# High and low parts of the attention values in one matmul of 130 columns

## The chip, the cores and the metric

The kernel runs on one core of a Trainium2 chip. The metric is the device time in microseconds (us) of one execution, given as the median of several runs. Four engines compute: TensorE (PE in the profile, its weight loads PEld), VectorE (DVE), ScalarE (ACT) and GpSimd (POOL). SyncE (SP) only issues DMAs.

## What is computed

Eight graphs of 2048 nodes, one layer of graph attention with 8 heads of 64 outputs, a residual and a layer norm:

```python
h = einsum('bnf,hfo->bhno', x, W)            # x: 8 x 2048 x 512, W: 8 x 512 x 64
s1 = einsum('bhno,ho->bhn', h, a1)
s2 = einsum('bhno,ho->bhn', h, a2)
e = leaky_relu(s1[..., :, None] + s2[..., None, :], negative_slope=0.2)
attn = softmax(where(adj > 0, e, -9e15), axis=-1)
out = layernorm(x + concat_heads(einsum('bhnm,bhmo->bhno', attn, h)))
```

Since exp(leaky_relu(s1+s2)) is a product of a factor of the row and a factor of the column on either side of s1+s2 = 0, the kernel needs no exponential per edge. It needs two masks per head, the edges with s1+s2 > 0 ("pos") and the other edges ("neg"), and multiplies each by a table with 65 columns per head: 64 scaled values and the denominator.

## The kernel before, in words

A **unit** is one head of one block of 512 rows. A batch has 4 blocks (k) of 8 heads (h), so 32 units, and there are 8 batches, 256 units in all. A unit has IT = 4 row tiles of 128 and JC = 16 column chunks of 128.

The tables exist as a high and a low f16 part, to keep precision: `b_hi`, `b_lo` for pos and `d_hi`, `d_lo` for neg.

What each engine does for a unit:

- **ScalarE** (L505 to L520, `compare`): copies the row scores to a PSUM bank (L510), then 13 comparisons of 128x512 (L519) into the two `step` tiles, 6 for the first half of the columns and 7 for the second. There is one pair of `step` tiles, so the comparisons of unit u+1 into a half begin when VectorE has used that half for unit u. In between it cuts adjacency pieces (L487, 8 per block: all in h = 0 of block 0, else two in h = 0 and one in h = 1 to 6) and copies transposed x tiles (L493, 16 per batch).
- **VectorE** (loop at L797 to L828): in iteration u it makes 3 comparisons (L707) and both masks of unit u+1: `make_pos` twice (L722, AND of half a mask), `make_neg` twice (L731, XOR of half a mask); then in some units a maximum (L567) or other small work; then `take_unit(u)` (L571 to L581): scale the neg sums out of PSUM (L576), add the pos sums (L579), invert the denominators (L581); then in h = 1 to 3 parts of the layer norm. Everything stands in this order in one queue. In unit 0 of a batch no masks are made (those of unit 1 were made in the batch's start).
- **TensorE** (L430 to L477): waits for the pos masks, and per row tile multiplies one tiny term (L448, 65 columns) and for each of 16 mask tiles the high part (L454) and the low part (L455), each a weight load of the mask tile and a matmul of 65 columns, all summed in the same 65 columns of a PSUM bank. Then in some units x transposes or score products (L368, L378, L386, L393, L399), then it waits for the neg masks and does the same without the tiny term (L475, L476). There are two sets of banks, by the parity of h, so pos of unit u+1 needs unit u-1 to have been read (`unit_read`).
- **GpSimd** divides the result of the unit by its denominator (L871, L876), adds x by DMA and does small parts of the norm.

A batch starts with 16 chunks of x times W (L429, f32), which VectorE scales and splits (L693 to L698) and GpSimd completes (L915, L917).

## Time and profile before

| | us |
|---|---|
| median of 3 runs | 3147.84 |
| lowest, highest | 3135.4, 3163.03 |
| the profiled execution's own time | 3138.42 |
| its span | 3136.7 |
| TensorE busy | 2744.1 |
| VectorE busy | 2522.8 |
| ScalarE busy | 2419.3 |
| GpSimd busy | 827.5 |

The span is counted from the first to the last instruction, the own time is that of the same execution as the runs measure it. "Busy" of TensorE is the union of matmuls that overlap one another, so a matmul's mean duration (195 ns) is far more than the distance between two of them. "issue" in a wait is time in which an engine waited for no semaphore that the profile shows. The mean granted clock of TensorE is 0.967 of full speed.

### The profile page before, as it was taken

To read this page: it belongs to the slowest core of one execution; us is meant where nothing else is said; L and a number is where in the kernel's file an instruction comes from. 1 tells how busy PE (TensorE), PEld (TensorE's weight loads), DVE (VectorE), ACT (ScalarE), POOL (GpSimd) and SP (SyncE) were. 2 spreads that over 40 slices of the span, in tenths; PEclk is the share of its full clock that TensorE was granted. 3 is DMA by queue.
4 is the path that set the end of the run, shared out by engine and by line. 5 is a ranking of instruction groups with operands and counts; after the bars stand their busy time and mean duration, and the time that the engine had idled before them with its cause. 6 is when DMAs were issued, how large, how long until landed. Compare 5 with 4: busy or idle time off the path is not lost.

```text
span 3136.7 us, 158793 instructions
## 1 busy us (share of the span) xinstructions
PE 2744.1 (87%) x68636; PEld 2398.0 (76%) x68636; DVE 2522.8 (80%) x3954; ACT 2419.3 (77%) x4029; POOL 827.5 (26%) x1011
## 2 busy tenths in 40 slices
PE   4898889998898898988989889998898888988886
PEld 2498876988678885888858888498884888758886
DVE  4888878887887878888788787888877877788876
ACT  2499973999658996599856998479973989739994
POOL 2522115111341113312142111521215111161211
PEclk9999999999999999999999999999999999999998
DMA  5357643576526655277442765437644556345753
GB/s 162 93 116 161 141 100 100 123 164 131 130 71 136 150 130 136 63 157 157 111 118 70 159 155 122 98 88 165 150 108 115 112 143 156 90 112 115 165 135 94
DMA packets 281338, 392.28 MB, mean 125 GB/s; under 512 B 161856, under 2 KB 161856, under 8 KB 280672
## 3 DMA queue, kind: packets, MB, share of 16 engines
q1 hardware_dynamic: 253536, 315.24, 39.9%
q0 software_dynamic: 27136, 67.12, 12.7%
q8 instruction: 545, 8.93, 1.2%
q14 instruction: 121, 0.99, 0.2%
HBM read 313.52 MB, written 34.14 MB: 111 GB/s over the span
## 4 chain that ended last, share of the span: by engine, by line
PE 67%; issue 13%; DVE 10%; ACT 7%; DMA 1%; SPq 1%; POOL 0%; DVEq 0%; ACTq 0%; POOLq 0%
PE ps L475 14%; PE ps L476 14%; PE ps L455 13%; PE ps L454 13%; PE ps L429 8%; ACT step L519 7%; PE ps L368 2%; DVE m_neg L731 1%; DVE y L603 1%; PE ps L386 1%; PE ps L399 1%; DVE prod L695 1%; PE ps L448 1%; DVE prod_d L698 1%; DVE m_pos L722 1%
## 5 line engine op out<-in xcount | busy, mean ns | idle before, releaser
L519 ACT ACTIVATE step<-ps,s_steep 128x512 fp8e4<-128x512 f32 x3328 | 1954.1, 726 | 289.7 <-DVE m_pos L722 246.9
L455 PE MATMUL ps<-b_lo,m_pos 128*128 128x65 f16 x16384 | 1094.3, 195 | 96.4 <-issue 95.4
L454 PE MATMUL ps<-b_hi,m_pos 128*128 128x65 f16 x16384 | 1093.7, 195 | 54.4 <-issue 36.5
L475 PE MATMUL ps<-d_hi,m_neg 128*128 128x65 f16 x16384 | 1071.9, 195 | 67.0 <-issue 61.2
L455 PEld LDWEIGHTS ps<-b_lo,m_pos 128*128 128x128 fp8e5 x16384 | 1052.3, 98 | 101.3 <-issue 101.0
L475 PEld LDWEIGHTS ps<-d_hi,m_neg 128*128 128x128 fp8e5 x16384 | 1043.6, 99 | 98.5 <-issue 97.9
L476 PE MATMUL ps<-d_lo,m_neg 128*128 128x65 f16 x16384 | 1072.7, 195 | 42.3 <-issue 42.1
L454 PEld LDWEIGHTS ps<-b_hi,m_pos 128*128 128x128 fp8e5 x16384 | 1052.5, 98 | 66.3 <-issue 66.1
L476 PEld LDWEIGHTS ps<-d_lo,m_neg 128*128 128x128 fp8e5 x16384 | 1039.1, 99 | 34.9 <-issue 33.3
L722 DVE TENSOR_TENSOR m_pos<-step,maskT 128x1024 uint32<-128x1024 uint32 x512 | 623.8, 1242 | 163.4 <-ACT step L519 130.6
L731 DVE TENSOR_TENSOR m_neg<-m_pos,maskT 128x1024 uint32<-128x1024 uint32 x512 | 602.8, 1217 | 0.0
L429 PE MATMUL ps<-W_sb,xT 128*128 128x512 f32 x1024 | 464.1, 615 | 61.5 <-DVE prod_d L698 54.7
L871 POOL TENSOR_TENSOR den_scaled<-den_inv,bound 128x4 f32<-128x4 f32 x256 | 74.9, 292 | 1592.0 <-DVE den_inv L581 1533.9
L429 PEld LDWEIGHTS ps<-W_sb,xT 128*128 128x128 f32 x1024 | 200.8, 198 | 319.3 <-issue 240.6
L707 DVE TENSOR_SCALAR step<-s_bc,s_neg 128x512 fp8e5<-128x512 f32 x768 | 391.1, 565 | 12.4 <-DVE s_neg L666 3.6
L487 ACT ACTIVATE adj_cut<-adj_in 128x1024 fp8e4<-128x1024 int32 x264 | 291.1, 1132 | 120.0 <-DMA adj_in<-in_adj 120.0
L576 DVE TENSOR_TENSOR neg_part<-ps,r_row 128x260 f32<-128x260 f32 x256 | 108.8, 425 | 316.3 <-PE ps L476 315.8
L493 ACT ACTIVATE xT<-ps 128x512 f32<-128x512 f32 x144 | 96.9, 673 | 175.8 <-PE ps L368 175.8
L510 ACT ACTIVATE ps<-s_bc 128x512 f32<-128x512 f32 x256 | 174.6, 682 | 71.9 <-DVE s_neg L666 71.4
L876 POOL TENSOR_TENSOR y<-total,den_scaled 128x256 f32<-128x256 f32 x256 | 206.2, 805 | 22.7 <-POOL den_scaled L871 2.3
L448 PE MATMUL ps<-tiny,ones_bf 128*128 128x65 bf16 x1024 | 199.0, 194 | 11.2 <-issue 6.3
L917 POOL TENSOR_TENSOR d_lo<-prod_d,d_hi 128x512 f16<-128x512 f32 x128 | 176.2, 1376 | 9.0
(81 smaller groups left out, 1703.4 us busy)
## 6 DMA issues: line engine op xcount, KB each, us to landing
adj_in<-in_adj SPq DMA_DIRECT2D x266, 512.0 KB, 4.8
s_bc<-s_rows SPq DMA_DIRECT2D x258, 256.0 KB, 3.8
x_in<-in_x SPq DMA_DIRECT2D x144, 256.0 KB, 4.7
x_sum<-in_x POOLq DMA_DIRECT2D x128, 256.0 KB, 4.6
y<-in_x POOLq DMA_DIRECT2D x32, 1024.0 KB, 10.4
out<-y SPq DMA_DIRECT2D x32, 1024.0 KB, 7.4
maskT<-adj_cut SPq DMA_TRANSPOSE x264, 4.3
W_sb<-in_L_gnn_W SPq DMA_DIRECT2D x4, 256.0 KB, 6.8
```

Source lines behind the costliest of these rows:

```text
L429: mm = pe.matmul(ps[:, H_BANKS[jc % 3], :], xT[:, fc, jc * P:(jc + 1) * P], W_sb[:, fc, :], start=(fc == 0), stop=(fc == FC - 1))
L448: pe.matmul(acc, ones_bf[:], tiny[:, h, :], start=True, stop=False)
L454: pe.matmul(acc, mask, b_hi[:, j, h, :], start=False, stop=False)
L455: mm = pe.matmul(acc, mask, b_lo[:, j, h, :], start=False, stop=(j == JC - 1))
L475: pe.matmul(acc, mask, d_hi[:, j, h, :], start=(j == 0), stop=False)
L476: mm = pe.matmul(acc, mask, d_lo[:, j, h, :], start=False, stop=(j == JC - 1))
L487: nc.scalar.activation(adj_cut8[slot][:], adj_in[slot][:], ACT.Relu, scale=STEEP, saturate=False).then_inc(adj_cut, 1)
L519: ins = nc.scalar.activation(chunk(step[qd], c, 0, BLK), ps[:, BANK_S1, :], ACT.Relu, bias=s2_steep[:, j, h:h + 1], scale=STEEP, saturate= ...
L707: ins = V.tensor_scalar(chunk(step[qd], c, 0, BLK).bitcast(FP8_WIDE), s1_bc[hp][:], s2_neg[:, j, h:h + 1], STEP_UP, ALU.is_gt, ALU.mult, s ...
L722: V.tensor_tensor(words(m_pos[hp][:, js, :]), words(step[qd][:]), words(mask[:, js, :]), ALU.bitwise_and).then_inc(pos_made, 1)
L731: V.tensor_tensor(words(m_neg[hp][:, js, :]), words(m_pos[hp][:, js, :]), words(mask[:, js, :]), ALU.bitwise_xor).then_inc(neg_made, 1)
L876: G.tensor_tensor(y[par][:, :, h * O:(h + 1) * O], total[hp][:, :, 0:O], den_scaled[hp][:].unsqueeze(2).to_broadcast([P, IT, O]), ALU.mult ...
```

## The change

High and low part of a table lie next to each other in one tile (`b_both`, `d_both`: 2 x 65 columns per head). One matmul of 130 columns per mask tile takes the place of two of 65, and leaves the high and the low sum in neighbouring slots of a PSUM bank. VectorE adds the two sums with a reduction over a pair whose members lie 65 elements apart: pos by `take_pos`, between the pos and the neg mask of the next unit, neg at the head of `take_neg`. Scaling and adding then run from SBUF. A bank holds two slots of 130 columns, so pos takes banks 0 and 1 and neg banks 2 and 3, one set for all units: pos of unit u+1 needs pos of unit u read (`pos_read`), likewise neg (`neg_read`). The neg mask is one XOR of 2048 words instead of two of 1024, at both places where it is made.

```diff
--- before
+++ after
@@ -110,10 +110,11 @@
         BANK_X = 6
-        b_hi = sb("b_hi", [P, JC, H, O1], F16)
-        b_lo = sb("b_lo", [P, JC, H, O1], F16)
-        d_hi = sb("d_hi", [P, JC, H, O1], F16)
-        d_lo = sb("d_lo", [P, JC, H, O1], F16)
+        b_both = sb("b_both", [P, JC, H, 2, O1], F16)
+        d_both = sb("d_both", [P, JC, H, 2, O1], F16)
+        b_hi, b_lo = b_both[:, :, :, 0, :], b_both[:, :, :, 1, :]
+        d_hi, d_lo = d_both[:, :, :, 0, :], d_both[:, :, :, 1, :]
         maskT = [sb(f"maskT{i}", [P, JC // 2, 2 * BLK], FP8) for i in range(2)]
         m_pos = [sb(f"m_pos{i}", [P, JC // 2, 2 * BLK], FP8) for i in range(2)]
...
@@ -222,10 +223,12 @@
         step_dve = sem("step_dve", free=1)
         pos_made = sem("pos_made", free=QUADS)
         neg_made = sem("neg_made", free=0)
+        pos_read = sem("pos_read", free=0)
+        neg_read = sem("neg_read", free=0)
         unit_done = sem("unit_done", free=1)
         pos_summed = sem("pos_summed", free=1)
         neg_scaled = sem("neg_scaled")
-        unit_read = sem("unit_read", free=1)
+        total_made = sem("total_made")
         den_inverted = sem("den_inverted")
         den_made = sem("den_made")
         att_made = sem("att_made", free=1)
...
@@ -244,6 +247,16 @@
         def pairs(ap):
             return ap.bitcast(BF16)
+        S = 2 * O1
+        def slot(bank, it):
+            return ps[:, bank + it // 2, it % 2 * S:(it % 2 + 1) * S]
+        def slots(bank):
+            return ps[:, bank:bank + 2, 0:2 * S].rearrange("p k (t l c) -> p k t c l", t=2, l=2)
         def chunk(tile, j, i0, n):
...
@@ -442,17 +455,19 @@
                             pe.wait_ge(lo_made, at(lo_made, 2 * JC * (b + 1) - 2))
                         pe.wait_ge(pos_made, at(pos_made, QUADS * (u + 1)))
-                        pe.wait_ge(unit_read, at(unit_read, u - 1))
+                        pe.sem_inc(waited[pe.engine], 1)
+                        pe.wait_ge(pos_read, at(pos_read, u))
+                        pe.sem_inc(waited[pe.engine], 1)
                         for it in range(IT):
-                            acc = ps[:, 2 * hp, it * O1:(it + 1) * O1]
-                            pe.matmul(acc, ones_bf[:], tiny[:, h, :], start=True, stop=False)
+                            acc = slot(0, it)
                             for j in range(JC):
                                 if unit == 0 and it == 0 and j == JC - 1:
                                     pe.wait_ge(lo_made, at(lo_made, 2 * JC * (b + 1) - 1))
                                     pe.sem_inc(waited[pe.engine], 1)
                                 mask = chunk(m_pos[hp], j, it * P, P).bitcast(FP8_WIDE)
-                                pe.matmul(acc, mask, b_hi[:, j, h, :], start=False, stop=False)
-                                mm = pe.matmul(acc, mask, b_lo[:, j, h, :], start=False, stop=(j == JC - 1))
+                                mm = pe.matmul(acc, mask, b_both[:, j, h, :, :], start=(j == 0), stop=(j == JC - 1))
+                                if j == 0:
+                                    pe.matmul(acc[:, 0:O1], ones_bf[:], tiny[:, h, :], start=False, stop=False)
                         mm.then_inc(pos_summed, 1)
                         if unit == 0:
                             pe.wait_ge(lo_made, at(lo_made, 2 * JC * (b + 1)))
...
@@ -466,14 +481,15 @@
                         if unit == STURN_UNIT:
                             turn_scores(b + 1)
                             mean_h(b + 1)
-                        pe.wait_ge(neg_made, at(neg_made, QUADS * (u + 1)))
+                        pe.wait_ge(neg_made, at(neg_made, u + 1))
+                        pe.sem_inc(waited[pe.engine], 1)
+                        pe.wait_ge(neg_read, at(neg_read, u))
                         pe.sem_inc(waited[pe.engine], 1)
                         for it in range(IT):
-                            acc = ps[:, 2 * hp + 1, it * O1:(it + 1) * O1]
+                            acc = slot(2, it)
                             for j in range(JC):
                                 mask = chunk(m_neg[hp], j, it * P, P).bitcast(FP8_WIDE)
-                                pe.matmul(acc, mask, d_hi[:, j, h, :], start=(j == 0), stop=False)
-                                mm = pe.matmul(acc, mask, d_lo[:, j, h, :], start=False, stop=(j == JC - 1))
+                                mm = pe.matmul(acc, mask, d_both[:, j, h, :, :], start=(j == 0), stop=(j == JC - 1))
                         mm.then_inc(unit_done, 1)
...
@@ -567,17 +583,23 @@
                 V.tensor_reduce(xmax[:, col:col + 1], x_in[slot][:], AX.X, ALU.max,
                                 apply_absolute_value=True).then_inc(x_maxed, 1)
-            def take_unit(u, h, it0):
+            def take_pos(u, h):
                 hp = h % 2
-                pos = ps[:, 2 * hp, 0:IT * O1].rearrange("p (t c) -> p t c", t=IT)
-                neg = ps[:, 2 * hp + 1, 0:IT * O1].rearrange("p (t c) -> p t c", t=IT)
+                dve.wait_ge(pos_summed, at(pos_summed, u + 1))
+                dve.wait_ge(att_made, at(att_made, u - 1))
+                dve.sem_inc(waited[dve.engine], 1)
+                V.tensor_reduce(total[hp][:], slots(0), AX.X, ALU.add).then_inc(pos_read, 1)
+            def take_neg(u, h, it0):
+                hp = h % 2
                 r = r_row[:, it0:it0 + IT, h:h + 1].to_broadcast([P, IT, O1])
                 dve.wait_ge(unit_done, at(unit_done, u + 1))
-                V.tensor_tensor(neg_part[:], neg, r, ALU.mult).then_inc(neg_scaled, 1)
+                V.tensor_reduce(neg_part[:], slots(2), AX.X, ALU.add).then_inc(neg_read, 1)
+                dve.wait_ge(neg_read, at(neg_read, u + 1))
+                V.tensor_tensor(neg_part[:], neg_part[:], r, ALU.mult).then_inc(neg_scaled, 1)
                 dve.wait_ge(neg_scaled, u + 1)
-                dve.wait_ge(att_made, at(att_made, u - 1))
-                V.tensor_tensor(total[hp][:], pos, neg_part[:], ALU.add).then_inc(unit_read, 1)
-                dve.wait_ge(unit_read, at(unit_read, u + 1))
+                V.tensor_tensor(total[hp][:], total[hp][:], neg_part[:], ALU.add).then_inc(total_made, 1)
+                dve.wait_ge(total_made, u + 1)
                 V.reciprocal(den_inv[hp][:], total[hp][:, :, O]).then_inc(den_inverted, 1)
             def ln_first_half(g, par):
...
@@ -722,27 +744,28 @@
                 V.tensor_tensor(words(m_pos[hp][:, js, :]), words(step[qd][:]),
                                 words(mask[:, js, :]), ALU.bitwise_and).then_inc(pos_made, 1)
-            def make_neg(u, h, mask, qd):
+            def make_neg(u, h, mask):
                 hp = h % 2
-                if qd == 0:
-                    dve.wait_ge(unit_done, at(unit_done, u - 1))
-                js = slice(qd * JQ // 2, (qd + 1) * JQ // 2)
-                dve.wait_ge(pos_made, at(pos_made, QUADS * u + qd + 1))
-                V.tensor_tensor(words(m_neg[hp][:, js, :]), words(m_pos[hp][:, js, :]),
-                                words(mask[:, js, :]), ALU.bitwise_xor).then_inc(neg_made, 1)
-            def make_masks(u, h, mask, nth, first_of_block=None):
+                dve.wait_ge(unit_done, at(unit_done, u - 1))
+                dve.wait_ge(pos_made, at(pos_made, QUADS * (u + 1)))
+                V.tensor_tensor(words(m_neg[hp][:]), words(m_pos[hp][:]), words(mask[:]), ALU.bitwise_xor
+                                ).then_inc(neg_made, 1)
+            def make_masks(u, h, mask, nth, first_of_block=None, before=None):
                 compare(h, nth)
                 for qd in range(QUADS):
                     make_pos(u, h, mask, qd, first_of_block)
-                for qd in range(QUADS):
-                    make_neg(u, h, mask, qd)
+                if before is not None:
+                    take_pos(u - 1, before)
+                make_neg(u, h, mask)
             V.nop().then_inc(x_maxed, start[x_maxed])
             V.nop().then_inc(step_dve, start[step_dve])
             V.nop().then_inc(pos_made, start[pos_made])
             V.nop().then_inc(neg_made, start[neg_made])
-            V.nop().then_inc(unit_read, start[unit_read])
+            V.nop().then_inc(pos_read, start[pos_read])
+            V.nop().then_inc(neg_read, start[neg_read])
             V.memset(ones_bf[:], 1.0).then_inc(ones_bf_made, 1)
             V.memset(wa[:], 0.0)
             V.memset(tiny_f[:], TINY * SPLIT_TOP).then_inc(setup_step, 1)
...
@@ -804,10 +827,13 @@
                             dve.sem_inc(waited[dve.engine], 1)
                             with dve.If(b < B - 1):
                                 make_masks(u + 1, 0, maskT[0], (g + 1) * (H // 2), g + 1)
+                            take_pos(u, h)
                         elif h == H - 1:
-                            make_masks(u + 1, 0, maskT[(k + 1) % 2], (g + 1) * (H // 2), g + 1)
+                            make_masks(u + 1, 0, maskT[(k + 1) % 2], (g + 1) * (H // 2), g + 1, before=h)
                         elif unit > 0:
-                            make_masks(u + 1, h + 1, maskT[k % 2], g * (H // 2) + (h + 1) // 2)
+                            make_masks(u + 1, h + 1, maskT[k % 2], g * (H // 2) + (h + 1) // 2, before=h)
+                        else:
+                            take_pos(u, h)
                         if unit in TILE_UNIT:
                             t = TILE_UNIT.index(unit)
                             max_x(JC * (b + 1) + t, t % 2, (b + 1) * (JC // 2) + t // 2, t)
...
@@ -823,7 +849,7 @@
                             no_edge_part(b + 1, 0)
                             no_edge_part(b + 1, 1)
                             no_edge_part(b + 1, 2)
-                        take_unit(u, h, k * IT)
+                        take_neg(u, h, k * IT)
                         for when, work in ((1, ln_first_half), (2, ln_statistics), (3, ln_apply)):
                             if h == when and k:
                                 work(g - 1, (k - 1) % 2)
```

VectorE, an iteration of the block loop that has a maximum in it, before (rows as the program lists them; ISA and REGISTER_ALU are waits and register steps of the queue):

```order
L722 TENSOR_TENSOR m_pos<-step,maskT 128x1024
L720 REGISTER_ALU
L722 TENSOR_TENSOR m_pos<-step,maskT 128x1024
L731 TENSOR_TENSOR m_neg<-m_pos,maskT 128x1024 x2
L566 ISA
L567 TENSOR_REDUCE xmax<-x_in 128x1
L576 TENSOR_TENSOR neg_part<-ps,r_row 128x260
L579 TENSOR_TENSOR total<-ps,neg_part 128x260
L581 RECIPROCAL den_inv<-total 128x4
```

The same place in the changed kernel:

```order
L744 TENSOR_TENSOR m_pos<-step,maskT 128x1024
L742 REGISTER_ALU
L744 TENSOR_TENSOR m_pos<-step,maskT 128x1024
L591 TENSOR_REDUCE total<-ps 128x260
L750 ISA
L751 TENSOR_TENSOR m_neg<-m_pos,maskT 128x2048
L582 ISA
L583 TENSOR_REDUCE xmax<-x_in 128x1
L597 TENSOR_REDUCE neg_part<-ps 128x260
L599 TENSOR_TENSOR neg_part<-neg_part,r_row 128x260
L601 TENSOR_TENSOR total<-total,neg_part 128x260
L603 RECIPROCAL den_inv<-total 128x4
```

Two reductions are new in the queue, one of them ahead of the XOR, and the two XORs are one.

TensorE, from the last pos matmuls of a unit with an x transpose to its first neg matmuls, before:

```order
L454 MATMUL ps<-b_hi,m_pos 128x65
L455 MATMUL ps<-b_lo,m_pos 128x65
L365 REGISTER_ALU
L368 MATMUL ps<-ident,x_in 128x128 x4
L469 REGISTER_ALU
L475 MATMUL ps<-d_hi,m_neg 128x65
L476 MATMUL ps<-d_lo,m_neg 128x65
```

The same place in the changed kernel, on to the next unit's pos:

```order
L470 MATMUL ps<-tiny,ones_bf 128x65
L468 MATMUL ps<-b_both,m_pos 128x130 x15
L378 REGISTER_ALU
L381 MATMUL ps<-ident,x_in 128x128 x4
L484 REGISTER_ALU
L492 MATMUL ps<-d_both,m_neg 128x130 x64
L457 ISA
L468 MATMUL ps<-b_both,m_pos 128x130
```

The pairs of 65 columns are single matmuls of 130, 64 for each mask of a unit; the tiny term now comes second in its row tile.

## Rows read from the trace of the kernel before

**Rows 1.** The page: span; busy us, share and instructions of each engine.

```profile
span 3136.7 us, 158793 instructions
PE 2744.1 (87%) x68636; PEld 2398.0 (76%) x68636; DVE 2522.8 (80%) x3954; ACT 2419.3 (77%) x4029; POOL 827.5 (26%) x1011
```

**Rows 2.** The page: shares of the chain of waits, by engine.

```profile
PE 67%; issue 13%; DVE 10%; ACT 7%; DMA 1%; SPq 1%; POOL 0%; DVEq 0%; ACTq 0%; POOLq 0%
```

**Rows 3.** Waits of the whole run: who for whom, us, times, longest.

```profile
DVE neg_part L576 <- PE ps L476: 315.8, 154, 8.2
...
ACT step L519 <- DVE m_pos L722: 246.9, 101, 15.8
...
DVE m_pos L722 <- ACT step L519: 130.6, 103, 2.9
...
PE ps L455 <- issue: 95.4, 75, 3.4
```

**Rows 4.** Windows of one batch: start, units 1-7 of block 0, blocks 1, 2, 3.

```profile
core 0: us, PE busy (x) PEld busy (x) DVE busy (x) ACT busy (x) POOL busy (x), PEclk, DMA share, GB/s
1208.97:1275.05 66.08, 58.28 (x132) 25.62 (x133) 56.52 (x96) 32.22 (x50) 41.22 (x35) 0.95 0.45 112
...
1287.16:1348.00 60.84, 59.62 (x1895) 59.20 (x1891) 55.19 (x79) 54.75 (x94) 10.33 (x18) 1.00 0.32 76
1348.00:1428.00 80.00, 67.71 (x2012) 66.31 (x2009) 63.68 (x95) 73.59 (x123) 15.57 (x23) 0.96 0.68 154
1428.00:1508.00 80.00, 69.98 (x2088) 68.51 (x2085) 65.17 (x99) 74.73 (x126) 15.66 (x23) 0.96 0.69 150
1508.00:1597.00 89.00, 81.49 (x2211) 72.98 (x2208) 68.04 (x118) 69.97 (x120) 14.36 (x20) 0.98 0.48 108
```

**Rows 5.** Timeline of VectorE, one unit of block 0: start us, us, instruction, idle before.

```profile
1295.67 0.43 DVE L576 TENSOR_TENSOR neg_part<-ps,r_row 128x260 f32<-128x260 f32 x1 [0.27 <-PE ps L476]
1296.13 0.43 DVE L579 TENSOR_TENSOR total<-ps,neg_part 128x260 f32<-128x260 f32 x1
1296.60 0.18 DVE L581 RECIPROCAL den_inv<-total 128x4 f32<-128x4 f32 x1
1296.73 1.64 DVE L707 TENSOR_SCALAR step<-s_bc,s_neg 128x512 fp8e5<-128x512 f32 x3
1298.51 2.36 DVE L722 TENSOR_TENSOR m_pos<-step,maskT 128x1024 uint32<-128x1024 uint32 x2
1300.79 2.35 DVE L731 TENSOR_TENSOR m_neg<-m_pos,maskT 128x1024 uint32<-128x1024 uint32 x2
1303.47 0.43 DVE L576 TENSOR_TENSOR neg_part<-ps,r_row 128x260 f32<-128x260 f32 x1 [0.33 <-PE ps L476]
```

**Rows 6.** Timeline of ScalarE in the same block.

```profile
1300.41 7.63 ACT L519 ACTIVATE step<-ps,s_steep 128x512 fp8e4<-128x512 f32 x13 [0.28 <-ACT ps L510]
1308.08 0.60 ACT L510 ACTIVATE ps<-s_bc 128x512 f32<-128x512 f32 x1
1308.96 7.63 ACT L519 ACTIVATE step<-ps,s_steep 128x512 fp8e4<-128x512 f32 x13 [0.28 <-ACT ps L510]
```

**Rows 7.** TensorE: two matmul groups of the page.

```profile
L454 PE MATMUL ps<-b_hi,m_pos 128*128 128x65 f16 x16384 | 1093.7, 195 | 54.4 <-issue 36.5
L448 PE MATMUL ps<-tiny,ones_bf 128*128 128x65 bf16 x1024 | 199.0, 194 | 11.2 <-issue 6.3
```

**Rows 8.** Windows of ten us in which TensorE stalled, recovered and ran full.

```profile
1130.00:1140.00 10.00, 6.54 (x183) 6.33 (x180) 5.81 (x6) 9.72 (x17) 2.19 (x3) 0.98 0.95 190
1140.00:1150.00 10.00, 9.89 (x192) 7.11 (x189) 8.16 (x14) 8.92 (x16) 0.81 (x2) 0.85 0.85 140
1150.00:1160.00 10.00, 10.00 (x333) 10.00 (x334) 5.73 (x11) 6.18 (x11) 0.82 (x2) 1.00 0.17 45
```

**Rows 9.** The page: the queue that brings instructions (packets, MB, share).

```profile
q8 instruction: 545, 8.93, 1.2%
```

**Rows 10.** Groups of VectorE reductions and f32 additions: busy us, mean ns.

```profile
L567 DVE TENSOR_REDUCE xmax<-x_in 128x1 f32<-128x512 f32 x144 | 97.6, 677 | 25.5 <-DMA x_in<-in_x 25.5
...
L657 DVE TENSOR_TENSOR tiny_f<-tiny_f,tiny_part 128x520 f32<-128x520 f32 x18 | 12.4, 692 | 0.0
...
L621 DVE TENSOR_REDUCE stat<-s_col 128x8 f32<-128x128 f32 x9 | 3.4, 373 | 1.1
...
L622 DVE TENSOR_REDUCE stat<-xmax 128x1 f32<-128x16 f32 x9 | 1.4, 158 | 0.0
...
L772 DVE TENSOR_REDUCE w_norm<-ps 128x1 f32<-128x512 f32 x1 | 0.7, 692 | 3.4 <-PE ps L412 3.4
```

**Rows 11.** Timeline of VectorE: masks over a batch's end, and its unit 0.

```profile
1212.51 1.22 DVE L722 TENSOR_TENSOR m_pos<-step,maskT 128x1024 uint32<-128x1024 uint32 x1 [2.94 <-ACT step L519]
1216.56 1.23 DVE L722 TENSOR_TENSOR m_pos<-step,maskT 128x1024 uint32<-128x1024 uint32 x1 [2.83 <-ACT step L519]
...
1287.20 0.43 DVE L576 TENSOR_TENSOR neg_part<-ps,r_row 128x260 f32<-128x260 f32 x1 [8.25 <-PE ps L476]
```

6 lines of the change are left out of this document (3 added, 3 removed).

## The prediction, made before the change was run

> **What bounds the kernel now.** I read the page first: TensorE is busy for 87% of the span, VectorE for 80%, ScalarE for 77% [rows 1], and the chain of waits runs through TensorE for 67% [rows 2]. So no engine has much room, and the question is which waits end last. The list of waits answers it: VectorE stands 315.8 us before `take_unit` for TensorE, and 130.6 us before the pos masks for ScalarE; ScalarE stands 246.9 us for VectorE's pos masks [rows 3]. The three form one loop. TensorE holds VectorE up in `take_unit`, and because that stands ahead of the next masks in VectorE's queue, ScalarE and then TensorE are held too.
>
> The windows show the loop by stage. In units 1 to 7 of a batch TensorE is busy for 59.62 of 60.84 us, VectorE for 55.19, ScalarE for 54.75. In blocks 1 to 3 TensorE does 67.71, 69.98 and 81.49 us in 80, 80 and 89, VectorE 63.68, 65.17 and 68.04 [rows 4]. TensorE's missing time there is stalls by "issue": 95.4 us before the low pos matmuls alone [rows 3], and they fall where DMAs are thick (183 matmuls in ten us at a DMA share of 0.95, against 333 at 0.17) [rows 8]. TensorE reads 8.93 MB of instructions through its own queue [rows 9], and I take late instructions for the cause.
>
> **What the change does to TensorE.** A full window holds 333 matmuls of 65 columns, 30.0 ns from one to the next [rows 8]; the mean of 195 ns in the groups is each one's way through the engine, several at once, and no cost [rows 7]. At 2.4 GHz (granted clock 1.00 in that row) 65 columns are 27.1 ns, so 2.9 ns is fixed. One matmul of 130 columns has as bounds 54.2 ns (no fixed part) and 60.0 (two of the old); I take 57.1. A unit of 260 x 30.0 = 7.8 us becomes 128 x 57.1 + 4 x 30.0 = 7.4 us: 0.4 us less. It has 132 weight loads and as many matmuls where there were 260 of each, so the stalls should about halve.
>
> On fetching, the Trainium skill (Runtime: NRT & Kernel Launch, Instruction fetch mechanics) says that instructions come in blocks of 16 KiB and that the cost is mostly hidden. The size agrees (8.93 MB in 545 packets), "hidden" does not agree with the 95.4 us in one line. By that rule the change would be worth 0.4 us a unit on TensorE at most.
>
> **What it does to VectorE.** Step by step for one unit:
>
> - *Two reductions added.* Each reads 520 f32 from PSUM and writes 260. A reduction of 512 costs 0.692 us from PSUM and 0.677 from SBUF [rows 10]; with 8 more elements I take 0.70. The lower bound is 520 elements at 1.04 ns, 0.54 us, and a small overhead: 0.60. The upper bound comes from the one reduction with far strides: 128 elements, 16 x 4 bytes apart, cost 373 ns, while 16 next to each other cost 158 [rows 10]. With an overhead of 158 - 16 x 1.04 = 141 ns that is 1.81 ns an element, and 520 of them cost 1.08 us. Pos is followed by an instruction that waits for nothing and starts some 0.08 us before its end (as the second XOR does: two of 1.22 us in 2.35), so it takes 0.62. Neg is followed by its reader: 0.70 + 0.04 = 0.74.
> - *Scale and add from SBUF.* Now 0.43 us each from PSUM [rows 5]. The f32 addition of 520 from SBUF costs 0.692 [rows 10], so 260 cost 0.42. Nothing gained or lost.
> - *One XOR for two.* The pair takes 2.27 us to the next start; one of 2048 words should take 1.22 + 1024 x 1.04 ns = 2.28 less the overlap of 0.08. Gain 0.07.
>
> The sum is 0.62 + 0.74 - 0.07 = **1.29 us a unit, 330 us in 256 units**. The pos reduction of a batch's unit 0 lies within a wait of 8.25 us [rows 11], so 5 us of it are free: 325.
>
> A unit of block 0 is 7.80 us from one `take_unit` to the next with 0.33 us of waiting [rows 5], so 7.47 of work; it becomes 8.76. ScalarE's own round there is 8.56 us (1300.41 to 1308.96) [rows 6], TensorE's 7.4 to 7.8. **VectorE becomes the bound.**
>
> **What of it is absorbed.** VectorE waits 315.8 + 130.6 = 446.4 us for TensorE and ScalarE now [rows 3]. Not all of that is open to it. In each batch 8.25 us before unit 0 is TensorE's work after a serial start, and 2.94 + 2.83 us at the end is ScalarE, which cannot begin unit 0 of the next batch before VectorE has its scores [rows 11]: 14.0 x 8 = 112 us stay. The other 334 us are waits that VectorE reaches later by the added work. Of them I leave 30 us standing, where block 3 has score products of 512 columns on TensorE (81.49 us busy [rows 4]) and ScalarE cuts two pieces. So 304 go, 325 come: +21 us. TensorE's unit 0 is shorter by 0.4 x 8 = 3: **+18 us**.
>
> The windows give the same from another side. Units 1 to 7 have 55.19 + 7 x 1.29 = 64.2 us of VectorE work and some 2 us of gaps, 66 for 60.84: 5 us longer. Block 1 has 63.68 + 10.3 + 4 of gaps = 78, block 2 79.5, for 80: 2.5 shorter. Block 3, 68.04 + 10.3 + 4 + 5.8 = 88 for 89: 1 shorter. That is 1.5 us a batch, 12 in all.
>
> The single bank set costs nothing in this: pos of unit u+1 now waits for `take_pos(u)`, 0.62 us behind the pos masks that it waits for anyway, and TensorE has over 1 us in each unit to give. Neg of unit u+1 needs `take_neg(u)`'s first reduction, 2.9 us behind that, and pos takes 3.7. Behind the waiting `take_pos` in VectorE's queue stands the XOR, which TensorE needs only after those 3.7 us.
>
> The profiled execution took 3138.4 us, 1.7 more than its span; with +18 it is 3156. The median of the runs stands 9.4 above it, so I forecast **3166 us**.
>
> **Rivals.**
>
> 1. *Balanced, as above*: 3166, 50%. Its own range is 3120 to 3215 (reductions 0.62 to 0.74, 0 to 80 us of waits left).
> 2. *The pair is slow to read*, 33%. The two members lie 65 elements apart, so no two successive reads are neighbours. At 1.08 us a reduction costs 0.38 more, twice a unit, 195 us, and since VectorE is the bound all of it is paid: 3361. For it speaks the reduction of 373 ns [rows 10]. Against it: that one reads SBUF, and no row shows a strided read of PSUM. It decides from 0.73 us a reduction, where the rise of 18 passes 31 us, 1%. The Trainium skill (SBUF — State Buffer, the note on cachelines) says that a stride past a line of 16 bytes pays a penalty in SBUF, and that PSUM has lines of 8 bytes, two f32. By it the pair would pay at every element; the SBUF row agrees, no row shows PSUM.
> 3. *Faster*, 12%. The stalls of TensorE spread further than the waits I counted: the small gaps between VectorE's instructions, about 4 us in a block, are partly waits too short to be listed. If half of them (2 x 4 x 8 = 64 us) and the 30 I left went as well, the result is 3072; half of that effect, 3120.
> 4. *TensorE's clock falls*, 5%. It idles over 1 us in every unit now. The clock fell to 0.85 on average in the ten us after a stall [rows 8]. At 1.2 GHz for a third of each unit TensorE needs about 9 us, and the six units of a batch with other TensorE work then come last, 1.5 us each: +72, 3238.
>
> The range reaches from part of 3 to the whole of 2: 3110 to 3375. What a measurement here can tell from no change is about 1%, 31 us. Of case 1's 50%, 28 lie within that, 3 below and 19 above; of case 3's 12%, 9 are faster and 3 within; of case 2's 33%, 3 are so cheap that they stay within, 30 are slower, as are the 5 of case 4. So faster 12%, same 34%, slower 54%. The likeliest case itself is "no change".
>
> **What would show it.** Right: VectorE busy at about 2850 us; its wait for TensorE before the neg reduction down to little more than 66 us (unit 0); TensorE busy shares down and its chain share taken by VectorE; matmuls of 130 columns 57 ns apart; instruction traffic near 5 MB; the reductions at 0.70 us. Units 1 to 7 longer, the later blocks not. Wrong: reductions of 1 us or more (case 2); VectorE still waiting some 200 us for TensorE, with TensorE full at a low granted clock (case 4); or a wait of TensorE for `pos_read` in every unit while VectorE itself waits for ScalarE, which would mean that the single bank set has closed a loop that I called open.

## The result: no change that lasts, where 18 us more were forecast

The changed kernel takes 3128.9 us (median of 13 runs, 3126.1 to 3131.6), the kernel before beside it 3147.8 (13 runs, 3120.7 to 3163.4): ratio 0.9948, 95% interval 0.9925 to 0.9971. In a second comparison on another occasion the changed kernel takes 3128.0 (12 runs), the kernel before 3130.5 (17 runs): ratio 1.0015, 0.9989 to 1.0041. So where both ran side by side the change is worth between half a per cent and nothing, and not the 0.6% more that I forecast. The changed kernel hardly moves from run to run; the kernel before does. Ratios leave out the runs that lie more than 1.5% above the fastest of their kernel (six of the 17 in the second comparison), so they can differ a little from the quotient of the medians. On a third occasion, on another chip than that of the second comparison, the kernel before took 3097.8 us and the changed kernel was not run; if it is as steady there as the version of experiment 8 was (3087.4 us there, 3089.2 on the later occasion), it would be about 1% slower than the kernel before. That is an estimate from these numbers.

The page of the changed kernel: span, busy us of each engine, the instruction queue, the chain's shares.

```profile
span 3127.7 us, 94002 instructions
...
PE 2628.9 (84%) x35868; PEld 2276.5 (73%) x35868; DVE 2821.2 (90%) x4210; ACT 2419.8 (77%) x4029; POOL 822.5 (26%) x1011
...
q8 instruction: 296, 4.85, 0.7%
...
DVE 42%; ACT 18%; issue 18%; PE 18%; DMA 1%; DVEq 1%; POOL 1%; SPq 1%; ACTq 0%; POOLq 0%
```

Against [rows 1] VectorE is busy 298.4 us more and TensorE 115 us less. Against [rows 2] the chain has passed from TensorE (67%) to VectorE (42%). The instruction queue brings 4.85 MB where it was 8.93 [rows 9]. The list of waits (who for whom, us, times, longest):

```profile
PE ps L468 <- DVE total L591: 325.9, 210, 3.9
...
DVE m_pos L744 <- ACT step L535: 65.7, 63, 2.9
...
DVE total L591 <- PE ps L468: 36.9, 8, 5.1
...
DVE neg_part L597 <- PE ps L492: 20.1, 9, 2.8
...
PE ps L468 <- issue: 0.4, 1, 0.4
...
PE ps L492 <- issue: 0.2, 1, 0.2
```

VectorE's waits of 315.8 and 130.6 us [rows 3] are now 36.9 + 20.1 and 65.7. TensorE waits 325.9 us for the pos sum to be read, which is the slack that it now has. And the line that I had misjudged: TensorE's waits by "issue" inside its attention matmuls were 95.4 us on one line [rows 3] and 235.2 on all four. These are the other three in the kernel before:

```profile
PE ps L475 <- issue: 61.2, 43, 2.8
...
PE ps L476 <- issue: 42.1, 32, 3.2
...
PE ps L454 <- issue: 36.5, 41, 2.3
```

In the changed kernel they are 0.4 + 0.2 us. They do not hide in the wait for the pos sum either: in each of the 216 units in which the trace has TensorE idle until that sum is read, its pos matmuls start 0.15 us after the reduction's end.

The new operations, by group (busy us, mean ns, idle before):

```profile
L744 DVE TENSOR_TENSOR m_pos<-step,maskT 128x1024 uint32<-128x1024 uint32 x512 | 620.4, 1242 | 96.3 <-ACT step L535 65.7
L751 DVE TENSOR_TENSOR m_neg<-m_pos,maskT 128x2048 uint32<-128x2048 uint32 x256 | 584.1, 2281 | 0.4
...
L591 DVE TENSOR_REDUCE total<-ps 128x260 f32<-128x520 f32 x256 | 177.4, 693 | 47.0 <-PE ps L468 36.9 <-issue 9.4 <-DVE s_neg L688 0.7
L597 DVE TENSOR_REDUCE neg_part<-ps 128x260 f32<-128x520 f32 x256 | 176.9, 691 | 20.3 <-PE ps L492 20.1
L599 DVE TENSOR_TENSOR neg_part<-neg_part,r_row 128x260 f32<-128x260 f32 x256 | 109.8, 429 | 8.7
```

And one unit of block 0 on VectorE's timeline, the answer to [rows 5]:

```profile
1305.34 0.69 DVE L597 TENSOR_REDUCE neg_part<-ps 128x260 f32<-128x520 f32 x1
1306.07 0.43 DVE L599 TENSOR_TENSOR neg_part<-neg_part,r_row 128x260 f32<-128x260 f32 x1
1306.53 0.43 DVE L601 TENSOR_TENSOR total<-total,neg_part 128x260 f32<-128x260 f32 x1
1307.00 0.18 DVE L603 RECIPROCAL den_inv<-total 128x4 f32<-128x4 f32 x1
1307.22 1.67 DVE L729 TENSOR_SCALAR step<-s_bc,s_neg 128x512 fp8e5<-128x512 f32 x3
1309.01 2.36 DVE L744 TENSOR_TENSOR m_pos<-step,maskT 128x1024 uint32<-128x1024 uint32 x2
1311.29 0.69 DVE L591 TENSOR_REDUCE total<-ps 128x260 f32<-128x520 f32 x1
1311.89 2.28 DVE L751 TENSOR_TENSOR m_neg<-m_pos,maskT 128x2048 uint32<-128x2048 uint32 x1
```

Both reductions take 0.69 us. From start to start neg costs 0.73, pos 0.60 and the XOR 2.20. From the neg reduction at 1305.34 to the end of the XOR there is no wait left; the queue is full.

By stage, from the reading of the neg sums of unit 0 to that of units 7, 15, 23 and 31 of one batch. Before (stretch, its length, then busy us and instructions of PE, PEld, DVE, ACT, POOL; granted clock, DMA share, GB/s):

```profile
1287.20:1346.95 59.75, 58.53 (x1858) 58.11 (x1855) 54.21 (x75) 53.70 (x92) 10.33 (x18) 1.00 0.31 74
1346.95:1429.46 82.51, 70.22 (x2094) 68.82 (x2091) 65.68 (x99) 76.10 (x128) 15.57 (x23) 0.96 0.68 154
1429.46:1510.05 80.59, 70.58 (x2106) 69.10 (x2103) 65.74 (x99) 75.05 (x126) 15.66 (x23) 0.96 0.69 149
1510.05:1602.02 91.97, 84.24 (x2155) 72.75 (x2151) 69.87 (x120) 72.93 (x124) 14.36 (x20) 0.98 0.47 106
```

After:

```profile
1287.32:1351.22 63.90, 57.17 (x991) 56.24 (x988) 62.08 (x82) 55.72 (x96) 10.86 (x19) 1.00 0.33 78
1351.22:1429.33 78.11, 64.13 (x1080) 62.90 (x1078) 74.93 (x108) 74.74 (x126) 15.56 (x23) 0.98 0.65 157
1429.33:1507.58 78.25, 64.80 (x1070) 63.58 (x1068) 75.17 (x108) 74.87 (x126) 15.64 (x23) 0.96 0.62 153
1507.58:1599.22 91.64, 78.76 (x1098) 67.62 (x1095) 79.24 (x128) 73.10 (x124) 13.61 (x20) 0.96 0.41 104
```

Block 0 (first rows) is 4.2 us longer: there nobody had time to give, and VectorE's 62.08 of 63.90 us is the bound. In this batch blocks 1 and 2 are 4.4 and 2.3 us shorter although VectorE does 9.3 and 9.4 us more in them, and block 3 is 0.3 shorter with 9.4 more. Over all eight batches the means are 3.5 longer, then 3.4, 0.9 and 1.4 shorter. The lengths of the first three stages vary in the kernel before (block 1 from 77.7 to 84.8 us) and are the same to 0.02 us in every batch of the changed kernel. In blocks 1 and 2 ScalarE is as busy as VectorE (74.74 and 74.93 of 78.11 us), so there the two are the bound together.

### The profile page after: what moved, and what is told of

It reads as the page before. It is cut to its first block, busy times and chain, and to the rows that moved or that the text cites. A ratio compares the mean times of both kernels' runs of the same rounds, so it can differ in the third digit from the quotient of the medians.

```text
span 3127.7 us, 94002 instructions
## 1 busy us (share of the span) xinstructions
PE 2628.9 (84%) x35868; PEld 2276.5 (73%) x35868; DVE 2821.2 (90%) x4210; ACT 2419.8 (77%) x4029; POOL 822.5 (26%) x1011
## 3 DMA queue, kind: packets, MB, share of 16 engines
q8 instruction: 296, 4.85, 0.7%
## 4 chain that ended last, share of the span: by engine, by line
DVE 42%; ACT 18%; issue 18%; PE 18%; DMA 1%; DVEq 1%; POOL 1%; SPq 1%; ACTq 0%; POOLq 0%
ACT step L535 16%; DVE m_neg L751 10%; PE ps L442 7%; DVE m_pos L744 6%; PE ps L468 5%; DVE step L729 5%; PE ps L492 4%; DVE neg_part L597 3%; DVE total L591 2%; DVE neg_part L599 2%; DVE total L601 2%; DVE y L625 2%; DVE xmax L583 1%; ACT ps L526 1%; DVE ln_stats L612 1%
## 5 line engine op out<-in xcount | busy, mean ns | idle before, releaser
L468 PE MATMUL ps<-b_both,m_pos 128*128 128x130 f16 x16384 | 1075.3, 228 | 348.2 <-DVE total L591 325.9
L468 PEld LDWEIGHTS ps<-b_both,m_pos 128*128 128x128 fp8e5 x16384 | 1020.9, 102 | 382.7 <-issue 382.7
L492 PE MATMUL ps<-d_both,m_neg 128*128 128x130 f16 x16384 | 978.4, 221 | 26.2 <-DVE neg_part L597 25.9
L492 PEld LDWEIGHTS ps<-d_both,m_neg 128*128 128x128 fp8e5 x16384 | 952.0, 98 | 41.4 <-issue 40.0
L744 DVE TENSOR_TENSOR m_pos<-step,maskT 128x1024 uint32<-128x1024 uint32 x512 | 620.4, 1242 | 96.3 <-ACT step L535 65.7
L751 DVE TENSOR_TENSOR m_neg<-m_pos,maskT 128x2048 uint32<-128x2048 uint32 x256 | 584.1, 2281 | 0.4
L591 DVE TENSOR_REDUCE total<-ps 128x260 f32<-128x520 f32 x256 | 177.4, 693 | 47.0 <-PE ps L468 36.9
L597 DVE TENSOR_REDUCE neg_part<-ps 128x260 f32<-128x520 f32 x256 | 176.9, 691 | 20.3 <-PE ps L492 20.1
L943 POOL TENSOR_TENSOR d_both<-prod_d,d_both 128x512 f16<-128x512 f32 x128 | 177.4, 1386 | 9.0
L941 POOL TENSOR_TENSOR b_both<-prod,b_both 128x512 f16<-128x512 f32 x128 | 144.0, 1125 | 108.5 <-DVE prod L717 106.3
L875 POOL DMA_DIRECT2D x_sum<-in_x x128 | 118.5, 926 | 107.6 <-DMA x_sum<-in_x 99.0
```

The source lines that it names most:

```text
L468: mm = pe.matmul(acc, mask, b_both[:, j, h, :, :], start=(j == 0), stop=(j == JC - 1))
L492: mm = pe.matmul(acc, mask, d_both[:, j, h, :, :], start=(j == 0), stop=(j == JC - 1))
L591: V.tensor_reduce(total[hp][:], slots(0), AX.X, ALU.add).then_inc(pos_read, 1)
L597: V.tensor_reduce(neg_part[:], slots(2), AX.X, ALU.add).then_inc(neg_read, 1)
L744: V.tensor_tensor(words(m_pos[hp][:, js, :]), words(step[qd][:]), words(mask[:, js, :]), ALU.bitwise_and).then_inc(pos_made, 1)
L751: V.tensor_tensor(words(m_neg[hp][:]), words(m_pos[hp][:]), words(mask[:]), ALU.bitwise_xor).then_inc(neg_made, 1)
```

## Experiments

Times are medians. The kernel before is given beside each group, because it is what varies: 3097.8 us (17 runs) beside the first group (the 65-column matmuls, the high sums alone, the late pos sum, GpSimd), 3135.3 (23 runs) beside the second (the second reduction, the two XORs, and the two made from the kernel before), 3130.5 (17 runs) beside the third. The changed kernel was 3128.9 and 3128.0 on its two occasions; differences from it are taken from 3128.5. The changed kernel did not run beside the first group. There the kernel before was 1% faster than elsewhere, so a version of the first group whose time moves as that of the kernel before does (experiment 1) may cost more elsewhere than its difference says.

**1. TensorE's relief taken back.**

```diff
-                                mm = pe.matmul(acc, mask, b_both[:, j, h, :, :], start=(j == 0), stop=(j == JC - 1))
+                            for l in range(2): for j in range(JC):    # neg likewise
+                                mm = pe.matmul(acc[:, l * O1:(l + 1) * O1], mask, b_both[:, j, h, l, :], start=(j == 0), stop=(j == JC - 1))
```

> The changed kernel, but each row tile first multiplies its 16 mask tiles by the high parts and then by the low parts, 65 columns each, into the same two slots: TensorE has 260 matmuls a unit again, VectorE's work is the changed kernel's. Theory (VectorE sets the pace; TensorE now has about 1.2 us of slack a unit, into which its instruction stalls fall): TensorE needs 7.8 us a unit and stalls for some 240 us in all again, so part of the stalls no longer fits: 3140 to 3175 us, and the runs spread over more than 10 us as those of before do, not over 5. Rival (the gain comes from VectorE's new order alone, one read of PSUM earlier, and the wide matmul brings nothing): 3129 us, spread 5 us.

Measured 3237.9 us (3219.2 to 3246.6), 109 more than the changed kernel; ratio to before 1.0435 (1.038 to 1.049). VectorE's work is the same (2824.5 us busy, 2821.2 in the changed kernel). Its waits:

```profile
PE ps L469 <- issue: 167.2, 113, 4.0
...
DVE neg_part L601 <- PE ps L495: 125.9, 59, 5.6
...
PE ps L495 <- issue: 81.9, 64, 4.2
```

The stalls are back (249 us on the two lines) and VectorE waits 125.9 us for the neg sums instead of 20.1. The wide matmul is what makes the change bearable. My theory (3140 to 3175) gave it 12 to 47 us and is far too low; the rival (nothing) is wrong. The likely reason is that a slack of 1.2 us a unit does not take in stalls of up to 4 us, and that VectorE's full queue cannot make up what it lost; no run here separates that.

**2. VectorE's load alone, without the relief.**

```diff
                 dve.wait_ge(unit_done, at(unit_done, u + 1))   # take_unit of the kernel before
+                for i in range(2): V.tensor_reduce(spare[i][:], both, AX.X, ALU.add)
```

> The kernel before with two idle reductions of 520 PSUM elements into spare tiles at the head of VectorE's reading of a unit: VectorE's added work of the change, 1.3 us a unit, without any of TensorE's relief. Theory (the wide matmuls make room for it, because TensorE's 7.8 us and its stalls are shorter): slower than the changed kernel by more than 30 us, 3160 to 3260 us. Rival (VectorE's waits would have absorbed the reductions anyway): 3130 to 3150 us.

Measured 3250.1 us (3236.5 to 3261.6), ratio to before 1.0363 (1.0313 to 1.0413).

```profile
DVE spare L579 <- PE ps L477: 178.5, 58, 8.2
...
PE ps L456 <- issue: 109.8, 64, 4.2
...
PE ps L476 <- issue: 54.1, 47, 2.8
...
PE ps L455 <- issue: 36.4, 35, 2.8
...
DVE r_row L675 <- issue: 31.3, 7, 5.2
...
PE ps L477 <- issue: 24.3, 28, 2.5
```

This version is 115 us or 3.6% above the kernel before, for 295.4 us more busy time on VectorE (2818.2), with 224.6 us of stalls on the four lines of TensorE. Not all of the 115 us is the load's work in the loop. VectorE itself stands 31.3 us by "issue" before `r_row` in the starts of seven batches, where the kernel before has 4.3, and the way from the last reading of a batch to the first of the next is 71.8 us instead of 66.9, 34 us in seven starts. The cause of that is open. The loop pays the rest, about 80 us or 2.6%. The step from here to the changed kernel is -122 us, and -88 without the 34; experiment 1, whose starts are as short as the changed kernel's, gives 109 us for the relief. So the two halves of the change are each about 3% of the time and cancel. They are not independent: experiment 6 has TensorE's relief and little more work on VectorE (60.9 us), and is only 1.6% below the kernel before.

**3. The pos reduction twice.**

```diff
+                V.tensor_reduce(spare[:], slots(0), AX.X, ALU.add)
                 V.tensor_reduce(total[hp][:], slots(0), AX.X, ALU.add).then_inc(pos_read, 1)
```

> The changed kernel with the reduction of the pos sums done twice (once into a spare tile). Adds 0.61 us a unit on VectorE and nothing elsewhere. Theory (VectorE sets the pace, all of its work is paid): 255 x 0.61 = 156 less 5 for unit 0 of each batch: 3270 to 3285 us. Rival (VectorE's waits or another engine's loop pace it, so half or more is absorbed): under 3210 us.

Measured 3241.8 us (3240.6 to 3243.3), 113 more. The rival falls, and the theory's 3270 to 3285 is missed too: of the 151 us of work three quarters are paid, not all. The stages say where: block 0 becomes 4.2 us longer (63.90 to 68.14 us), which is all of 7 x 0.61; blocks 1 and 2 become 3.9 and 3.7 longer and block 3 2.4, each of 8 x 0.61 = 4.9 (means of eight batches).

**4. The XOR in halves again.**

```diff
-                V.tensor_tensor(words(m_neg[hp][:]), words(m_pos[hp][:]), words(mask[:]), ALU.bitwise_xor).then_inc(neg_made, 1)
+                for qd in range(QUADS): ins = V.tensor_tensor(... the half qd of each ..., ALU.bitwise_xor)
+                ins.then_inc(neg_made, 1)
```

> The changed kernel with the XOR in two halves again, signalled once. Theory: 0.07 us a unit more on VectorE, all paid: 3129 + 18 = 3147 us. Rival (the size of the XOR does not matter): 3129.

Measured 3140.1 us (3135.7 to 3142.8), 12 more: two thirds of what I had expected (18), though VectorE is busy 23 us more (2844.4).

**5. One XOR in the kernel before**, the edit of `make_neg` alone.

> The kernel before with one XOR a unit and nothing else of the change. Theory (there TensorE and its stalls set the pace): 0 to 10 us less than before, within its noise. Rival (VectorE was the bound before too): 18 us less.

Measured 3134.9 us (3120.5 to 3152.2), ratio to before 1.0004 (0.997 to 1.0039). Neither the theory nor the rival is tested by it, because the edit shortens nothing on VectorE: it is busy 2526.2 us, 3.4 more than in the kernel before. The one XOR here follows directly on the AND whose result it reads. It cannot start before the AND's end, while the first of two XORs, which reads the first AND's half alone, started 0.08 us before it. In the changed kernel the pos reduction stands between the two, and the gain of 0.07 us is real.

**6. No second sums to read.**

```diff
-                V.tensor_reduce(total[hp][:], slots(0), AX.X, ALU.add).then_inc(pos_read, 1)
+                V.tensor_copy(total[hp][:] ..., high(0)).then_inc(pos_read, 1)
-                V.tensor_reduce(neg_part[:], slots(2), AX.X, ALU.add).then_inc(neg_read, 1)
-                V.tensor_tensor(neg_part[:], neg_part[:], r, ALU.mult).then_inc(neg_scaled, 1)
+                V.tensor_tensor(neg_part[:] ..., high(2), r ..., ALU.mult).then_inc(neg_read, 1)
```

> The changed kernel, but VectorE reads the high sums alone (a copy of 260 elements for pos, the scaling straight from PSUM for neg); the low sums are computed and left out of the result. VectorE loses about 1.0 us a unit, TensorE nothing. Theory (VectorE sets the pace): it becomes faster until ScalarE is the bound, whose own work is 8.6 to 10.7 us a unit: 14 to 20 us a batch less, 2970 to 3020 us. Rival (the single set of banks and TensorE's wait for the pos sum set the pace): under 1% less, above 3100 us.

Measured 3050.7 us (3049.0 to 3053.0), 78 less than the changed kernel, ratio to before 0.9838 (0.9792 to 0.9885). VectorE is busy 237.5 us less (2583.7), and a third of it shows. The time lies between the theory (2970 to 3020) and the rival (above 3100), and both are missed. ScalarE takes over (46% of the chain), as expected, at 368.5 us a batch (mean distance between the readings of the units 0), and it does not run full:

```profile
DVE m_pos L746 <- ACT step L538: 224.6, 185, 2.9
```

That wait is 65.7 us in the changed kernel. With VectorE and ScalarE this close, either waits for the other in turn, and neither runs full.

**7. The pos sum behind the XOR.**

```diff
-                if before is not None: take_pos(u - 1, before)
                 make_neg(u, h, mask)
+                if before is not None: take_pos(u - 1, before)
```

> The changed kernel, but VectorE sums pos of a unit behind the XOR of the next unit and not ahead of it: TensorE's pos matmuls wait 2.2 us longer for their banks. Theory (TensorE's wait for the banks lies in its slack): 3129 to 3140 us, TensorE's wait for the pos sum still near 330 us or up by less than 100, since its start is only shifted. Rival (the single set of banks is what paces the loop): up by a good part of 248 x 2.2 = 545 us, over 3300 us.

Measured 3159.4 us (3158.1 to 3162.3), 31 more. TensorE's wait for the banks:

```profile
PE ps L468 <- DVE total L591: 359.9, 216, 3.9
```

The rival (over 3300) falls, and the theory's "3129 to 3140" is too low. TensorE waits 34 us more for its banks, but VectorE's own queue accounts for the 31 us without that:

```profile
L751 DVE TENSOR_TENSOR m_neg<-m_pos,maskT 128x2048 uint32<-128x2048 uint32 x256 | 586.6, 2291 | 8.6
```

The XOR now stands behind the AND that it reads and starts 0.03 us after its end (8.6 us of idle time, 0.4 in the changed kernel), where the pos reduction and the XOR each started 0.08 us before the end of their predecessors. VectorE is busy 21.9 us more (2843.1) and has 8.6 us more of such gaps, 30.5 in all. So the place of the pos sum ahead of the XOR is worth 1%, as filler between an instruction and its reader; that the single bank set costs anything is not shown.

**8. Scaling, adding and the reciprocal on GpSimd.**

```diff
 take_neg (VectorE), after the reduction into neg_part[hp]:
-                V.tensor_tensor(neg_part, neg_part, r, mult); V.tensor_tensor(total, total, neg_part, add); V.reciprocal(den_inv, ...)
 divide_unit (GpSimd), at its head:
+                G.tensor_tensor(neg_part[hp][:], neg_part[hp][:], r, ALU.mult); G.tensor_tensor(total[hp][:], total[hp][:], neg_part[hp][:], ALU.add)
+                G.tensor_tensor(den_inv[hp][:], total[hp][:, :, O], minus_one[:], ALU.pow)
```

> The changed kernel, but GpSimd scales the neg sums, adds them to the pos sums and takes the reciprocal (as a power of -1), with two buffers for the neg sums and the row factors copied behind chunk 3 of a batch's start. VectorE loses some 1.1 us a unit, GpSimd gains 3 of 10 us a unit. Theory (VectorE sets the pace): 2970 to 3040 us, if GpSimd's reads do not slow VectorE's masks. Rival A (bank set paces): above 3100. Rival B (GpSimd and VectorE share a path to SBUF, so the masks of 1.22 us become longer by what GpSimd reads meanwhile, some 1 us a unit): 3110 to 3200 us, with the AND and XOR means up.

> Scaling, adding and the reciprocal on GpSimd once more, now beside the changed kernel: theory 30 to 50 us below it.

Measured 3087.4 us (3082.9 to 3092.0), ratio to before 0.9959 (0.9931 to 0.9986), and beside the changed kernel 3089.2 (3087.2 to 3097.2), ratio to before 0.9862 (0.9824 to 0.9901). It is the fastest version that computes the whole result, 41 us under the 3128.5 the first time and 39 under the changed kernel beside it the second time. The theory (2970 to 3040) is missed, as are rival A (above 3100) and the time of rival B (3110 to 3200); "30 to 50 us below" for the repetition holds. VectorE is rid of three operations a unit and yet busy only 138 us less (2682.9 in the second profile, from which these rows are):

```profile
L736 DVE TENSOR_TENSOR m_pos<-step,maskT 128x1024 uint32<-128x1024 uint32 x512 | 650.3, 1287 | 192.5 <-ACT step L536 160.8 <-DVE step L721 2.0
...
L721 DVE TENSOR_SCALAR step<-s_bc,s_neg 128x512 fp8e5<-128x512 f32 x768 | 471.9, 670 | 4.7 <-DVE s_neg L682 3.5
```

The comparisons of 566 ns now take 670 and the masks of 1242 ns take 1287: 80 and 30 us of busy time given back (rival B, in part). In the same trace a comparison during which GpSimd computes nothing takes 482 ns, one that runs mostly beside GpSimd's new addition takes 912. The Trainium skill (SBUF — State Buffer, SBUF: two separate sides) says that VectorE and GpSimd share a port pair, and that in certain cases (a VectorE instruction in a two-port mode or with two SBUF inputs) whichever starts first keeps it for a whole instruction; the rows show the lengthening and not who was blocked.

**9. The same with a fourth comparison on VectorE**, `DVE_SLOTS = {0: (6, 7), 1: (6, 7)}`.

> The same with a fourth of the 16 comparisons of a unit moved from ScalarE to VectorE. In the version on GpSimd ScalarE holds 41% of the chain and VectorE waits 162.5 us for it. Theory: ScalarE loses 0.57 us a unit, VectorE gains 0.55 to 0.65: 0 to 40 us below the version with three. Rival (VectorE is as near the bound as ScalarE, so it only swaps places): the same or up to 40 us above.

Measured 3101.5 us (3096.9 to 3103.4), 12 above the version with three. The rival holds: ScalarE's busy time falls by 144 us to 2271.7, VectorE's rises to 2768.6, and the bound only changes place (VectorE 47% of the chain, ScalarE 7%, where ScalarE had 36 to 41%).

**10. The kernel before with small adjacency loads.**

```diff
-                sp.dma_start(adj_in[slot][:], adj_tiles[..., slot * JH * P:(slot + 1) * JH * P]...)
+                n = P     # inside the batch loop; JH * P = 8 P in the start
+                sp.dma_start(adj_in[slot][:, 0:n], adj_tiles[..., slot * JH * P:slot * JH * P + n]...)
```

> The kernel before, but the adjacency loads inside the batch loop bring an eighth of their bytes (the rest of each piece is old data, so the edges are not the reference's); number and order of instructions stay. Theory (TensorE stalls inside its matmul groups, 190 times for 279 us, because its instructions come late when the DMA engines are full): stalls under 100 us, time 3020 to 3090 us, runs close together. Rival (the stalls belong to TensorE's 260 weight loads a unit, wherever the DMAs are): stalls stay above 200 us, time within 1% of before.

This version leaves out seven eighths of each adjacency piece inside the batch loop. Measured 3050.5 us (3044.8 to 3053.9), ratio to before 0.973 (0.9692 to 0.9768). The same instructions, weight loads and matmuls as before, 198 MB instead of 315 on the load queue:

```profile
DVE neg_part L577 <- PE ps L477: 129.3, 76, 8.2
...
PE ps L456 <- issue: 40.1, 44, 3.1
...
PE ps L455 <- issue: 24.9, 34, 2.2
PE ps L476 <- issue: 19.2, 19, 3.2
...
PE ps L477 <- issue: 8.6, 12, 1.4
```

92.8 us by "issue" on these lines instead of 235.2 (in 191 waits; the 279 of the expectation is not what the list says), and VectorE's wait for TensorE 129.3 instead of 315.8. The theory holds. With the weight loads and the instruction bytes unchanged, the stalls fall with the DMA traffic; halving the instructions takes them away altogether (changed kernel). Not all of the 80 us need be the stalls': ScalarE's wait for adjacency pieces falls too, from 120.0 to 78.8 us.

Where the stalls lie says what they are. TensorE's trace of the kernel before has 138,778 instructions, 255 for each of the 545 packets of [rows 9]. Counted in order of time, 198 instructions inside the attention matmuls start more than 0.3 us after the one before; from one of these to the next the count is an exact multiple of 256 in 174 of 197 cases (in experiment 1 in 164 of 187, here in 100 of 118). TensorE stops where a new packet of instructions begins. So the late instructions, argued in the prediction, are shown.

**11. The changed kernel again.**

> The changed kernel itself, on the chip of the three runs beside it, since the kernel before took 3098 us (median) beside one group of runs and 3135 beside another. Theory (what varies is how late TensorE's instructions come, and the changed kernel is nearly free of that): its own runs stay within 8 us of each other, near 3129 us, while those of before spread over 30 or more. Rival (chips differ in speed whatever the kernel): it moves by the same per cent as before does.

Measured 3128.0 us (3124.6 to 3134.0) against 3128.9: it does not move with the kernel before, which was 3147.8 and 3130.5. Spread of the runs, largest less smallest: kernels with 260 matmuls a unit 25 us (load alone), 27 (relief taken back), 32 (one XOR) and 43 to 60 (before); kernels with 132 from 3 (pos twice) to 10 (6 to 23 runs each). The small loads bring the kernel before to 9.

## Why the prediction was wrong, step by step

The step that failed is the sum on VectorE's queue: 325 us of added work, less 304 of absorbed waits, less 3, gave +18, and came out at -9. The 9.4 us of scatter set on top of it failed as well. Behind most of it stands one thing: I let TensorE's stalls halve, and they vanished.

- **What bounded the kernel before**: right in the main. TensorE's late instructions held the loop, and experiment 10 shows it: fewer DMA bytes, fewer stalls, 80 us less. What I passed over is ScalarE: in block 2 it was busy for 74.9 of 79.1 us already (mean of the batches), more than TensorE (68.7), so little could be gained there. (Its own round in block 0 is 8.55 us by [rows 6], not 8.56.)
- **VectorE becomes the bound**: right for block 0; in blocks 1 and 2 it shares the place with ScalarE (chain: VectorE 42%, ScalarE 18%). The reduction over far members costs 0.69 us, where I had taken 0.70. Case 2 is out. The Trainium skill (SBUF — State Buffer, the note on cachelines) gives PSUM lines of 8 bytes and says that reading it out of order slows matmuls; I had carried that over to VectorE. For VectorE's read the trace shows no such price: 520 elements, no two successive ones neighbours, cost no more than the 512 in a row of [rows 10].
- **The sum's first term failed: +325 us, or 330 of work.** The page gives 298.4 us more busy time (the 5 us that I took off for the units 0 are busy too). Starts and ends in the two traces give the 32 us between. Start to start the new work is 0.60 + 0.73 - 0.07 = 1.26 us a unit (timeline above) against 1.29: 8 us. Of the 0.73, 0.03 is the gap behind the neg reduction, which is idle and not busy: 9 us. An instruction that need not wait starts some 0.08 us before its predecessor's end, and when the wait before the neg reading went, the reading overlapped the XOR or the maximum before it for 17.0 us in all instead of 6.1: 11 us. The last 4 lie between other instructions that no longer wait. I had counted the waits without these overlaps.
- **The second term, -304 us of waits and -3 of unit 0**: all idle time of VectorE fell by 307.4 us (613.9 to 306.5). Right in size, though not in its reason: the listed waits fell by 317, and gaps of some 0.03 us between dependent instructions grew by 8. I wrote that the stalls "should about halve"; they went from 235.2 to 0.6 us, and I left 30 us of waits in block 3 that were hardly there, while ScalarE's waits of 65.7 stayed instead of 46. In the profile the balance is thus -9.0 us where I had +18.
- **The last step failed as well: 9.4 us carried over.** I set the forecast above the profile by what the kernel before's median had above its own profiled run. That was its scatter, which goes with stalls that the changed kernel does not have: its median lies 1.2 us above its span. 27 us of the sum and 10 of this are the 37 us between 3166 and 3129.
- **The price of VectorE's work as a whole** was right only because the relief came with it. Without it the work costs some 80 us in the loop (experiment 2), and 113 of 151 are paid for one more reduction in the changed kernel (3). Where VectorE alone is the bound, in block 0, such work is paid in full; where ScalarE is as near it, in part.
- **The single bank set costs nothing**: no run speaks against it. TensorE does wait for the pos sum in 210 of 256 units, which I had named as a sign of a closed loop, but VectorE is not waiting for ScalarE at the same time (65.7 us in all), and with the sum 2.2 us later the loop loses no more than VectorE's own queue explains (7). A second bank set was not tried.
- **Case 3, faster**, had the right sign and the wrong mechanism: not short unlisted waits, but stalls that vanish. Case 4 did not occur: the mean granted clock went from 0.967 to 0.959 only, and VectorE's wait for TensorE is 57 us, not some 200.
- **The range** held the time. "Within 1%", which came, had 34%; 54% lay on slower, 30 of them for a cost of reading PSUM that no row showed. That the time came so near to no change was foreseen as a balance, but the balance met had other weights; the nearness of the number is in part luck.

What stays open: whether it is the bytes of the instruction stream or the time left until the next packet is due that takes the stalls away. An estimate speaks for the time: 256 instructions are 128 matmuls and their weight loads, 128 x 30.0 = 3.8 us of TensorE's work before [rows 8] and 128 x 56 = 7.2 us now. Each packet has 3.4 us more, and the longest stall of the kernel before was 3.4 us. In the changed kernel bytes and time changed together; short matmuls with idle instructions between them, or wide ones with twice the instruction bytes, were not tried.

## What to carry to other kernels

Look at the waits by "issue" of a TensorE that runs many short matmuls beside heavy DMA traffic: here they were late instructions, in pieces of up to 4 us where a new packet of instructions begins, and halving the instructions removed them altogether. Count the instructions between two stalls: a fixed multiple tells. What the relief frees is worth only what the neighbours in the loop can take: here two halves of about 3% cancelled, and the next step was to unload the new bound (experiment 8, -39 us). Between an instruction and its reader, put one that depends on neither (experiment 7, 31 us). And when a kernel's runs scatter by 1% or more, do not carry the scatter into a forecast for a version that removes what goes with it.

## Seen of the hardware, not expected

- TensorE's stalls by "issue" go with the DMA traffic: 235.2 us at 315 MB on the load queue, 92.8 at 198 MB, same instructions. They lie whole multiples of 256 instructions apart in 174 of 197 cases.
- They fall from 235.2 to 0.6 us when the instruction traffic falls from 8.93 to 4.85 MB, and the scatter of the runs from over 40 us to under 10.
- A VectorE reduction of 520 f32 in PSUM over pairs 260 bytes apart takes 0.69 us, as one over 512 in a row; a matmul of 130 f16 columns with its weight load follows the last one in 56 ns, where two of 65 took 60 [rows 8]. TensorE's timeline of the changed kernel shows it: from the first row's start to the last row's lie 16 of 130 columns and one of 65, 0.93 us, less 0.03 for the latter.

```profile
1303.46 1.07 PE L468 MATMUL ps<-b_both,m_pos 128*128 128x130 f16 x16
1304.36 0.19 PE L470 MATMUL ps<-tiny,ones_bf 128*128 128x65 bf16 x1
1304.39 0.39 PE L468 MATMUL ps<-b_both,m_pos 128*128 128x130 f16 x4
```

- With three more operations a unit on GpSimd, VectorE's comparisons grow from 566 to 670 ns, 912 beside the addition.
- A VectorE instruction that reads its predecessor's result starts 0.03 us after that one's end, an independent one 0.08 us before it (8.7 us of idle time behind 256 neg reductions; 20 us of overlap behind 240 pos reductions).
